# Attention in 64-row fp32r tiles, with the causal mask added by TensorE

## The reference

```python
qkv = x @ W_qkv + b_qkv
q = _apply_rope(q, cos, sin); k = _apply_rope(k, cos, sin)
att = jnp.einsum('bhqd,bhkd->bhqk', q, k) / jnp.sqrt(jnp.float32(HS))
att = jnp.where(causal, att, jnp.float32(-1000000000.0))
att = jax.nn.softmax(att, axis=-1)
y = jnp.einsum('bhqk,bhkd->bhqd', att, v)
...
x = _layernorm(x + attention(x)); x = _layernorm(x + experts(x))
```

## Time and profile before

| | us |
|---|---|
| median of 3 runs (range) | 1476.37 (1474.4 to 1476.71) |
| profiled execution: time | 1476.77 |
| its span | 1475.0 |
| TensorE matmul busy | 1285.9 (87%) |
| VectorE busy | 1199.3 (81%) |
| ScalarE busy | 799.0 (54%) |
| GpSimd busy | 275.8 (19%) |

### The profile page before, as it was taken

How to read it: one execution, slowest core, us unless ns; L and a number is a source line. 1 busy time by engine, 2 the same in 40 slices (tenths; PEclk the granted TensorE clock), 3 DMA queues, 4 the chain that set the end, 5 groups by cost and what they waited for, 6 DMA issues and landing times. The chain is left out here.

```text
span 1475.0 us, 23637 instructions
## 1 busy us (share of the span) xinstructions
PE 1285.9 (87%) x7857; PEld 652.1 (44%) x7857; DVE 1199.3 (81%) x2812; ACT 799.0 (54%) x1130; POOL 275.8 (19%) x282
## 2 busy tenths in 40 slices
PE   5775369999999999999999999999577839999997
PEld 3443112333333333333333333332266629999997
DVE  5997679999999989999999999994077637888886
ACT  3443303666666666666666666667444434544542
POOL 3554430011010010110010100101233420211121
PEclk9888656999999999999999999999888759999999
DMA  4579474313113112131131130000345521324330
GB/s 148 163 205 257 142 123 69 71 35 87 31 30 87 31 54 62 31 85 32 54 91 31 29 88 9 14 10 9 123 141 173 186 89 65 122 95 147 97 97 24
DMA packets 119107, 126.72 MB, mean 86 GB/s; under 512 B 15452, under 2 KB 101599, under 8 KB 119008
## 3 DMA queue, kind: packets, MB, share of 16 engines
q1 hardware_dynamic: 115424, 117.00, 28.3%
q0 software_dynamic: 3584, 8.47, 1.6%
HBM read 83.02 MB, written 48.38 MB: 89 GB/s over the span
## 5 line engine op out<-in xcount | busy, mean ns | idle before, releaser
L656 ACT ACTIVATE probs<-scores 128x1024 f32<-128x1024 f32 (+3 forms) x640 | 538.9, 894 | 320.7 <-PE scores L549 319.8
L711 DVE TENSOR_REDUCE part_max<-ring 128x1 f32<-128x512 f32 x768 | 478.3, 684 | 24.4 <-PE ring L579 22.8
L579 PE MATMUL ring<-k_stack,q_stack 96*128 96x512 bf16 (+3 forms) x1280 | 406.9, 364 | 45.4 <-DMA k_stack<-pieces_d 30.4
L549 PE MATMUL scores<-q_stack,k_stack 99*128 99x512 bf16 (+3 forms) x1280 | 339.4, 350 | 2.4 <-ACT probs L656 1.6
L565 PE MATMUL out_p<-probs,v_s 128*32 128x512 f32 (+3 forms) x2560 | 299.9, 541 | 0.5 <-POOL probs L761 0.3
L579 PEld LDWEIGHTS ring<-k_stack,q_stack 96*128 96x128 bf16 x1280 | 115.1, 97 | 350.5 <-DVE part_max L711 147.5
L761 POOL TENSOR_SCALAR_AFFINE_SELECT probs<-probs 128x512 f32<-128x512 f32 x128 | 81.2, 634 | 773.9 <-ACT probs L656 773.9
L705 DVE CUSTOM_DVE_ANT_0 scratch<-ring,mask_s 128x384 f32<-128x384 f32 (+2 forms) x384 | 195.0, 550 | 17.2 <-issue 16.5
L549 PEld LDWEIGHTS scores<-q_stack,k_stack 99*128 99x128 bf16 x1280 | 113.0, 98 | 175.4 <-issue 65.0
L195 PE MATMUL psP<-xT,wqk_s 128*128 128x512 f32 x128 | 71.6, 723 | 35.4 <-ACT xT L234 31.4
L1425 PE MATMUL psY<-w_hi,h_hi 128*128 128x256 f32 x320 | 91.1, 285 | 0.0
(11 more groups left out here) (116 smaller groups left out, 1501.3 us busy)
## 6 DMA issues: line engine op xcount, KB each, us to landing
w_whole<-w SPq DMA_DIRECT2D x16, 1024.0 KB, 7.4
q_stack<-pieces_d SPq DMA_DIRECT2D x192, 64.0 KB, 2.9
k_stack<-pieces_d SPq DMA_DIRECT2D x192, 64.0 KB, 3.0
v_d<-vt SPq DMA_DIRECT2D x8, 1024.0 KB, 4.4
v_s<-v_d SPq DMA_DIRECT2D x8, 1024.0 KB, 6.0
o_d<-o_s SPq DMA_DIRECT2D x32, 256.0 KB, 2.2
p_o<-o_d SPq DMA_DIRECT2D x8, 1024.0 KB, 5.8
slots_d<-no_row SPq DMA_DIRECT2D x1, 5200.0 KB, 32.1
```

The lines of the kernel that those rows point to most:

```text
L549: last = nc.tensor.matmul(scores[p][:, hh, off:CHUNK], k_stack[i][0:KROWS, kb // TPC, j, kb % TPC * P:(kb % TPC + 1) * P], q_stack[i][0:KR ...
L579: last = nc.tensor.matmul(slot[:, h * w:(h + 1) * w], q_stack[i][0:SROWS, qt // TPC, j + h, qt % TPC * P:(qt % TPC + 1) * P], k_stack[i][0 ...
L656: nc.scalar.activation(probs[n % NPROB][:, 2 * p:2 * p + 2, off:CHUNK], scores[p][:, :, off:CHUNK], ACT.Exp, scale=SCALE).then_inc(exp_don ...
L711: nc.vector.tensor_reduce(part_max[:, qt, j, t:t + 1], ring[m % 3][:, 0:w], axis=AX.X, op=ALU.max).then_inc(ring_read, 1)
```

## The change

Scores and maxima use three products instead of six: q and k are cut into two fp32r pieces, so that a head has 48 rows, and 50 with two rows of the maximum. Two heads lie one in rows 0 to 63 and one in rows 64 to 127 of the stacks, and their matmuls use the upper and the lower half of TensorE's rows. Score matmuls are always 512 columns wide. On the diagonal the mask is added on TensorE, by two matmuls of 128 columns for each head (halves of an identity times halves of the mask, 64 rows each), and VectorE takes maxima alone, with one instruction for two heads where two blocks fit in 512 columns. A lone head's block on the diagonal is computed 512 wide. A unit has 148 items instead of 156. The step's order is two items, both score pairs, the other items, PV. The constants for the mask are loaded in 8 transfers behind the first chunk's 12 and rounded by one ScalarE copy; the rows of ones are loaded by 8 transfers instead of GpSimd's memset; the maxima of a chunk are stored by 4 transfers instead of 3. In `project_qkv` the middle piece, VectorE's `rest` and ScalarE's `cut_mid` go; GpSimd subtracts `hi` from `raw`, and the pieces are stored as two 4-byte tensors of 1 MB a chunk instead of three of 0.5 MB.

```diff
-TERMS = [(0, 0), (0, 1), (1, 0), (1, 1), (0, 2), (2, 0)]
+TERMS = [(0, 0), (0, 1), (1, 0)]
 NTERM = len(TERMS)
 SROWS = NTERM * HS
-NPIECE = 3
+NPIECE = 2
 KROWS = SROWS + NPIECE
 HPU = 4
+HALF = P // 2
+NPAIR = HPU // 2
...
-        hi = [sb(f"hi{i}", [P, QKG, CHUNK], BF16) for i in range(2)]
-        mid = [sb(f"mid{i}", [P, QKG, CHUNK], BF16) for i in range(2)]
-        low = [sb(f"low{i}", [P, QKG, CHUNK], BF16) for i in range(2)]
+        hi = [sb(f"hi{i}", [P, QKG, CHUNK], F32R) for i in range(2)]
+        low = [sb(f"low{i}", [P, QKG, CHUNK], F32R) for i in range(2)]
...
+                if g == 0:
+                    act.wait_ge(low_ready, QKG * (n + 1))
...
-            def rest(b, c, g):
-
-                i, done = c % 2, QKG * (NCH * b + c) + g + 1
-                dve.wait_ge(hi_ready, done)
-                dve.wait_ge(roped, done)
-                nc.vector.tensor_tensor(rots[i][:, g, :], raw[i][:, g, :], hi[i][:, g, :],
-                                        ALU.subtract).then_inc(rest_ready, 1)
...
-                pool.wait_ge(mid_ready, QKG * n + g + 1)
-                nc.gpsimd.tensor_tensor(low[i][:, g, :], rots[i][:, g, :], mid[i][:, g, :],
+                pool.wait_ge(hi_ready, QKG * n + g + 1)
+                nc.gpsimd.tensor_tensor(low[i][:, g, :], raw[i][:, g, :], hi[i][:, g, :],
...
-                if w == P:
-                    block += [(qt, t, j, 2, w, True) for j in range(0, HPU, 2)]
+                if 2 * w <= CHUNK:
+                    block += [(qt, t, half, 2, w, True) for half in range(2)]
...
-    cost = [1.2 if isinstance(item, int) else 0.08 + 0.08 * item[5] + item[3] * item[4] * (1 + (item[3] > 1)) / 960
-            for item in ITEMS]
+    cost = [0.7 if isinstance(item, int) else 0.08 + item[3] * item[4] / 960 for item in ITEMS]
...
-        N_LOAD = 2 * NTERM
-        MAX_DMAS = 16 * NPIECE
+        N_LOAD = 2 * NTERM * 2
+        MAX_DMAS = 16 * 2 * NPIECE
...
-                    rows = slice(r * HS, (r + 1) * HS)
-                    for stack, side, piece in ((q_stack, 0, qp), (k_stack, 1, kp)):
-                        sp.dma_start(stack[i][rows, c],
-                                     pieces_d[b, piece, side, g, :, :, cols]).then_inc(stack_loaded[i][c], 16)
+                    for par in range(2):
+                        rows = slice(par * HALF + r * HS, par * HALF + (r + 1) * HS)
+                        for stack, side, piece in ((q_stack, 0, qp), (k_stack, 1, kp)):
+                            sp.dma_start(stack[i][rows, c].bitcast(F32),
+                                         pieces_d[b, piece, side, g, par, :, :, cols]).then_inc(stack_loaded[i][c], 16)
...
+                n = NMAXROW // 2
                 for pc in range(NPIECE):
-                    sp.dma_start(q_stack[i][SROWS + pc:SROWS + pc + 1, c], max_rows[c][pc][:]).then_inc(max_loaded[c], 16)
+                    for par in range(2):
+                        row = par * HALF + SROWS + pc
+                        sp.dma_start(q_stack[i][row:row + 1, c].bitcast(F32),
+                                     max_rows[c][pc][par * n:(par + 1) * n, :].bitcast(F32)
+                                     ).then_inc(max_loaded[c], 16)
+
+            def load_ones(i):
+                for pc in range(NPIECE):
+                    for par in range(2):
+                        row = par * HALF + SROWS + pc
+                        sp.dma_start(k_stack[i][row:row + 1].bitcast(F32), ones_s[:]).then_inc(ones_loaded, 16)
...
-            sp.dma_start(mask_s[:], causal).then_inc(const_loaded, 16)
             sp.dma_start(id_s[:], ident).then_inc(const_loaded, 16)
-            for c in ORDER:
+            load_chunk(0, 0, 0, NCH - 1)
+            for par in range(2):
+                tile_rows = slice(par * HALF, (par + 1) * HALF)
+                for half, rows in enumerate((slice(0, HALF), slice(HALF, P))):
+                    sp.dma_start(half_in[tile_rows, half], ident[rows]).then_inc(half_loaded, 16)
+                    sp.dma_start(half_in[tile_rows, 2 + half], causal[rows]).then_inc(half_loaded, 16)
+            for c in range(NCH - 2, -1, -1):
                 load_chunk(0, 0, 0, c)
             load_v(0, 0, 0)
+            sp.wait_ge(ones_set, 1)
+            for i in range(2):
+                load_ones(i)
...
-                c, kb, off = STEPS[n]
+                c, kb, _ = STEPS[n]
                 pe.wait_ge(exp_done[p], NSTEP * u + n)
                 for hh in range(2):
-                    j = 2 * p + hh
-                    last = nc.tensor.matmul(scores[p][:, hh, off:CHUNK],
-                                            k_stack[i][0:KROWS, kb // TPC, j, kb % TPC * P:(kb % TPC + 1) * P],
-                                            q_stack[i][0:KROWS, c, j, off:CHUNK],
+                    rows = slice(hh * HALF, hh * HALF + KROWS)
+                    last = nc.tensor.matmul(scores[p][:, hh, :],
+                                            k_stack[i][rows, kb // TPC, p, kb % TPC * P:(kb % TPC + 1) * P],
+                                            q_stack[i][rows, c, p, :],
...
-                if not (isinstance(u, int) and u == 0 and m < 3):
-
-                    pe.wait_ge(ring_read, NRING * u + m - 2)
-                slot = ring[m % 3][:, 0:heads * w]
+                at = NRING * u + m
+                if at >= 3:
+
+                    pe.wait_ge(ring_read, at - 2)
+                span = w if heads > 1 else CHUNK
+                slot = ring[at % 3][:, 0:heads * span]
+                tile_rows = slice(j % 2 * HALF, (j % 2 + 1) * HALF)
+                rows = slice(j % 2 * HALF, j % 2 * HALF + SROWS)
                 for h in range(heads):
-                    last = nc.tensor.matmul(slot[:, h * w:(h + 1) * w],
-                                            q_stack[i][0:SROWS, qt // TPC, j + h, qt % TPC * P:(qt % TPC + 1) * P],
-                                            k_stack[i][0:SROWS, t, j + h, 0:w], start=True, stop=True)
+                    pair = j // 2 + h
+                    last = nc.tensor.matmul(slot[:, h * span:(h + 1) * span],
+                                            q_stack[i][rows, qt // TPC, pair, qt % TPC * P:(qt % TPC + 1) * P],
+                                            k_stack[i][rows, t, pair, 0:span], start=True, stop=not diag)
+                    if diag:
+                        if at == 0:
+                            pe.wait_ge(half_rounded, 1)
+                        for half in range(2):
+                            last = nc.tensor.matmul(slot[:, h * span + w - P:h * span + w], id_half[tile_rows, half],
+                                                    mask_half[tile_rows, half], start=False, stop=(half == 1))
...
-                second, third = min(first + 1, stop), min(first + 3, stop)
+                second = min(first + 2, stop)
+                items(u, i, uses, first, second, ahead)
                 chunk_waits(u, n)
-                score_pair(u, i, n, 0)
-                items(u, i, uses, first, second, ahead)
-                score_pair(u, i, n, 1)
-                items(u, i, uses, second, third, ahead)
+                for p in range(2):
+                    score_pair(u, i, n, p)
+                items(u, i, uses, second, stop, ahead)
                 if behind:
                     pv_step(*behind)
-                items(u, i, uses, third, stop, ahead)
...
+            act.wait_ge(half_loaded, 16 * 8)
+            nc.scalar.activation(halves[:], half_in[:], ACT.Copy).then_inc(half_rounded, 1)
...
-                if heads > 1:
-                    first = scratch[:, j, 0:heads * w].rearrange("p (h w) -> p h w", h=heads)
-                    pairs = 2 * NCH * u + 2 * (NCH - 1 - t) + j // 2
-                    dve.wait_ge(pair_read, 1 + pairs)
-                    dve.wait_ge(ring_full, NRING * u + m + 1)
-                    nc.vector.tensor_tensor(first, ring[m % 3][:, 0:heads * w].rearrange("p (h w) -> p h w", h=heads),
-                                            mask_s[:, CHUNK - P:CHUNK].unsqueeze(1).to_broadcast([P, heads, P]),
-                                            ALU.add).then_inc(ring_read, 1)
-                    dve.wait_ge(ring_read, NRING * u + m + 1)
-                    nc.vector.tensor_reduce(part_max[:, qt, j:j + heads, t], first, axis=AX.X,
-                                            op=ALU.max).then_inc(pair_read, 1)
-                elif diag:
-                    full = in_register(dve, NRING * u + m + 1)
-                    read = in_register(dve, NRING * u + m - 3) if m > 3 else None
-                    dve.wait_ge(const_loaded, 16 * 2)
-                    dve.wait_ge(ring_full, full)
-                    if m > 3:
-                        dve.wait_ge(ring_read, read)
-                    nc.vector.tensor_tensor_reduce(out=scratch[:, j, 0:w], in0=ring[m % 3][:, 0:w],
-                                                   in1=mask_s[:, CHUNK - w:CHUNK], scale=1.0, scalar=LOWEST,
```

(22 more changed lines are left out.)

78 lines of the change are left out of this document (32 added, 46 removed).

## The result

| | before | after |
|---|---|---|
| median of 4 runs (range) | 1475.89 (1474.4 to 1476.71) | 1498.43 (1492.02 to 1501.38) |
| profiled execution: time, span | 1476.77, 1475.0 | 1500.32, 1498.2 |

The ratio of the medians is 1.0149, with an interval of 1.0121 to 1.0176. I had forecast 1465. In one experiment, PV in two blocks, one run of the four (1587.13 us) took over 1.5% more than that kernel's fastest, and its ratio leaves it out. First the page of the changed kernel: the totals, the granted clock in 40 slices, and the costliest groups of attention (busy us, mean ns | idle before, and what ended it).

A forecast was written before the change was run, and what follows sets the result against it. TensorE was taken as the bound, VectorE 3% behind. From 1476.8 us, projection -9, start of attention +7 and the attention units -10 gave 1465; its own range was 1440 to 1490, the range for all cases 1405 to 1535.

The forecast's parts named there:

- the narrow rival: Mask matmuls on the diagonal: 128-column 4-byte matmuls cost the four-pass price, 0.213 us each; 1523 us, chance 0.22.
- no overlap: Scores and maxima on TensorE: the two row halves don't work at the same time; unit 119 us, total 1598, chance 0.15.
- Off the diagonal: Attention's maxima off the diagonal: VectorE becomes the bound, 59.5 us a unit with coupling, before 63.8.
- The diagonal: Attention's blocks on the diagonal: TensorE stays late, each goes from 9.75 to 10.5 us, 42 a unit.
- Mask matmuls at the bf16 price: Mask matmuls on the diagonal cost 0.055 us each; unit 96 us, total 1421, chance 0.14.
- Scores: TensorE's scores in attention: 160 matmuls a unit become 80 overlapping pairs of 0.22 to 0.23 us, 18.4 at most.
- Projection: Projection before attention: VectorE loses 32 subtractions, part of the gain is waited out; -9 us, bounds 0 and -18.
- Start of attention: First loads and first maxima of attention: extra transfers and TensorE at 1.2 GHz; +7 us, bounds 0 and +10.
- The tail: After the last fold: TensorE's scores and PV fall from 1.97 to 1.55 us a step, ScalarE keeps the tail's length.

The follow-up runs named there:

- the shorter reductions: The changed kernel with VectorE's reductions off the diagonal reading only the first 256 of 512 keys, TensorE's work untouched: 1439.99 us.
- the bf16 run: The changed kernel with pieces, stacks, maxima's rows and mask halves in bf16 instead of fp32r, same matmuls: 1408.75 us.
- the narrow run: The changed kernel with score matmuls on the diagonal as wide as before (384, 256, 128) instead of always 512: 1488.06 us.

## Why the prediction was wrong

The range held the time, 1498 in 1405 to 1535; the sign was wrong, and the odds were near even (0.51 to 0.42). That the range held was luck: the forecast's own range ended at 1490, and the upper end came from the narrow rival (1523), whose mechanism the runs refute. With it and "no overlap", the other slower rival, gone, none of the reasons that I had for a slower kernel is the one that made it slower.

- **The step that failed is "Off the diagonal"**: "A planned step holds 4.2 items, 2.5 us; PV, 1.09, fits in the two full buffers that DVE then has (1.2), just. I take 59.5 for coupling". The part took 66.8 us, and 59.5 was the term that was too small. I held the supply of DVE against PV alone. But DVE has to bridge PV's 1.00, the way into it with its open 4-byte load (0.43) and the way out to the first result (0.53), 1.96 us in all, and it has three buffers, of which the first becomes free only when DVE has read it. The loop of 2.70 us, shown by the shorter reductions, is the bound of the full steps, against 4 x 0.598 = 2.39 of DVE. It stands in ten steps of a unit; at 0.62 a maximum, as in my 59.5, they would take 2.48 each, so it makes 2.2 of the 7.3 us. The rest lies in spans that hold maxima of the diagonal too, or PV's other widths, and isn't taken apart here. The unit is 106.3 for 101.5: over 7.6 units that is 36 us, more than the whole error of 33. Some 8 us more are the dips of the clock and the first unit, which I had not in the sum.
- **Where much of the size came from** is the load. I had a price for it (0.115) and used it on the diagonal only, for the mask. Off the diagonal I let 4-byte maxima and scores pass at 0.22 or less. Against the bf16 run there are 0.11 more behind the first load after PV and 0.11 more behind the load out of a wait, 0.21 a step, and 4.5 us of the 7.3 in the whole part off the diagonal. The other 2.8 stay with bf16 pieces (62.3 for 59.5).
- **The diagonal** was off the other way: 39.5 us for my 42, 9.9 a clump for my 10.5, and 9.08 in the last one. The rival "Mask matmuls at the bf16 price" had 9.1, which fits the last clump and not the mean. A row of the changed kernel with two lone heads and four mask matmuls shows where my price was too high, 0.51 us (438.71 to 439.22) for which I had 0.70:

```profile
438.71 0.51 PE L585 MATMUL ring<-k_stack,q_stack 48*128 48x512 f32 x2
439.05 0.34 PE L592 MATMUL ring<-halves 64*128 64x128 f32 x4
439.22 0.69 PE L550 MATMUL scores<-q_stack,k_stack 50*128 50x512 f32 x4
```

  Lone heads of unlike parity load and multiply side by side, masks too: four mask matmuls pass in 0.17 us. The two heads of a paired item lie in the same half, and there the starts are the 0.11 apart that I had for the load:

```profile
461.77 0.27 PE L585 MATMUL ring<-k_stack,q_stack 48*128 48x128 f32 x1
461.88 0.39 PE L592 MATMUL ring<-halves 64*128 64x128 f32 x2
```

  My sum had used the overlap for the maxima and not for the masks of the lone heads. The rival was near in the clump and still far off in its time (1421): it took over my 59.5. Against the sign of my forecast stood not one of the rivals' mechanisms, but the term that all of them but "no overlap" shared.
- **Scores**: the halves overlap, so "no overlap" fell; and narrow 4-byte matmuls aren't at the four-pass price, so that rival fell too. Of the Trainium skill's two rules, TensorEngine Tiling (Array Packing), section Key Properties, that tiles load and multiply independently, now has its row: 448.43 to 448.91 for four scores. And the Trainium skill's other rule, TensorE: Matmul & The Clock Gate, section Weight-path perf modes, that 4-byte weights get no fast load, is the one that spoke against this change: 0.18 against 0.09 in the two kernels' rows. I had cited it and let it weigh on the diagonal alone. Widening the scores to 512 I had counted as a smaller saving only; the narrow run puts 2.3 us a unit on it.
- **Projection**: -19.5 for my -9, outside of my bounds (0 to -18). DVE's stretch fell by 24.7 us, of which the subtraction is 23.0; the rest of the pipeline followed nearly in full. I had let the chain behind ScalarE keep 0.9 us a chunk, and gave 7 us to the slots' transfer and the stores. Of these only a part is seen: DVE waits 12.3 us in all for V's projection, 5.6 before.
- **Start of attention**: 5.9 for my 7. The first maximum is 15.33 us behind the block's start (11.49 before), +3.8 for my 3.5, behind the 8 extra transfers, on ScalarE:

```profile
176.64 0.63 ACT L685 ACTIVATE halves<-half_in 128x512 fp32r<-128x512 f32 x1 [24.06 <-DMA half_in<-causal]
```

  Without mask matmuls the first maximum came 9.6 us behind the block's start, so the masks' constants are what it waits for. The first block of maxima is as long as before (37.2 against 37.4), where I had +3.5; PE is busy for all of it. 2.2 us lie behind the fold, which I had not in the sum.
- **The tail** grew by 3.7 us, where I had nothing. ScalarE isn't a full cover: it stood 2.62 us at one place. The granted clock dips there too: its mean behind the last fold is 0.92, where it was 1.00 before. With the old order of the step, the same 4-byte loads and a clock of 1.00, the tail takes 38.8 us, where the changed kernel has 42.0 and the kernel before 38.2. So some 3 of the 3.7 us are the clock's.

By the measured terms, 1476.8 - 19.5 + 5.9 + 36.2 + 0.5 = 1499.9, against 1500.3 of the profiled execution.

## What to carry to other kernels

When two engines share a few buffers, lay out the loop before adding up each engine: from the start of the block that uses no buffer, to the first result, through the consumer, to the producer that waits for that slot, and back. If the sum is more than either engine's own work, the loop is the bound of that step, and the busy shares (98% and 82% here) tell nothing; changing one term of it tells the rest. Then count in how many steps it stands: here it was ten of 40, and in others DVE alone was the bound. A 4-byte weight load shows where no long matmul runs in front of it, behind a wait, behind PV or between matmuls of 128 columns: cutting 96 rows to 48 paid here only with 2-byte pieces. The last block of a unit stood for all four in my reading, and in the changed kernel it is the shortest of them: measure each. A price read off the trace belongs in every place where the instruction stands, not just where it is new.

## What the chip showed that I had not expected

- **TensorE's clock fell to half in two edits and nearly in a third.** With all row work in one half, PE was busy for 1699 of 1700 us and the granted clock was 0.50; with PV in one pass it was 0.50 over 975 us, busy 972.49, and with bf16 pieces besides 0.53. The changed kernel, whose PE looks no busier by the records, is at 0.98 from the first exponential to the last, the kernel before at 1.00. A full busy row is thus no promise of 2.4 GHz. Which property of the work decides it these runs don't separate: the kernels without mask matmuls and with narrow scores have less work for PE as well, and were at 0.96 and 0.99. It belongs into the risk of an edit to TensorE's work: where 90 to 130 us less were expected, PV in one pass took 135 more.
- **Short dips** of 3.4 or 6.8 us at 1.2 GHz came in some units and not in others with the same instructions, up to 2.4 us a unit (108.64 and 108.68 against 106.32). The four runs of the changed kernel order by it: 1492 us at a mean clock of 0.926, 1497 at 0.925, 1500 at 0.921, 1501 at 0.919. Why they come these runs don't show.
- **A mask through TensorE is cheap where heads of both halves alternate**: four 128-column fp32r matmuls with their loads pass in 0.17 us there, and start 0.11 apart where one half does them alone. On average it is 0.052 us each, which for 1024 of them still makes 48 us.
